# First experts of a decoder kernel: the norm of four tiles in two parts, and the shared up weights split in four pieces

## The chip, the cores and the metric

The kernel runs on one core of a Trainium2 chip. The time is the device time of the whole kernel in microseconds (us). TensorE multiplies 128-row tiles and writes to the accumulator memory PSUM (`PS` in the program, eight banks of 128x512 fp32); VectorE (DVE), ScalarE (ACT) and GpSimd (POOL) do the elementwise work; SyncE (SP) starts the DMA transfers. Each engine runs its own instruction list in order, and engines wait for each other on semaphores.

## The reference, cut to what matters

A decoder of two layers on 2048 rows of 512 features. Every sublayer is added to its input and normalised. The change lies in the third sublayer, the first experts:

```
probs = softmax(xt @ w_router);  top 4 of 128 experts
basis = silu(xt @ w_gate) * (xt @ w_up)          # 8 bases of 256
mixed = sum over the bases, weighted by the chosen experts
out   = mixed @ w_down
shared = (silu(xt @ shared_w_gate) * (xt @ shared_w_up)) @ shared_w_down
x = layernorm(x + out + shared)
```

Matrix products have to keep fp32 accuracy. So each operand is split in a high part, rounded to the format that TensorE takes, and a low part, the rest; a product is three matmuls (high by high, high by low, low by high).

## The kernel before, in words

`xN` holds the 2048 rows as 16 tiles of 128x512. Each sublayer is a function that returns one instruction list for each engine; `Norm` builds the layer norm for a group of tiles, with `st`, `mv`, `nv`, `ny`, `nc_` as small tiles of statistics that all norms share.

In the first experts the 8 bases go over 16 tiles each (128 "tile" steps, line 1123 on TensorE). Base k's weights are fetched to `sg[k % 2]` and split into `WH[k % 2]` by one ACT instruction (`split_w`, L1232) and into `WL[k % 2]` by one POOL instruction (L1400). The shared gate weights are k = 8, the shared up weights k = 9. `WH[1]` and `WL[1]` are in use by base 7 until its last matmul, so the split of the up weights can start no earlier than that.

Then the shared part goes over the 16 tiles. For each tile t TensorE runs, in this order:

- T(t): transposes of `mixed` (L1203) and of the shared product in `s2` (L1206) to PSUM;
- S(t+1): 12 matmuls of shared gate and 12 of shared up for the next tile (L1192);
- O(t): 18 matmuls of the down projection (L1219), which read `tH` and `tL`.

ACT copies T(t) into the high part `tH` (L1286, L1288), runs the silu of S(t+1) (L1278), and after tiles 3, 7, 11 and 15 applies the norm to four tiles (`apply_act`, L186). DVE writes the low part `tL` (L1380, L1383), the product with the shared up half (L1371), and adds O(t) to `xN` (L1390). After tiles 3, 7, 11 and 15 it works out the norm at once (`all_dve`): four statistics (L137), four aggregates (L141), two small operations (L145, L149), three Newton rounds of three small operations (L156, L157, L159) and the hand-over `nc` (L170), each small one waiting for the one before. ACT and DVE take their lists in order, so what stands behind the norm there, the copies and the low part of the next tile, waits for it. The order is written out by hand in the loops; PSUM banks are handed out by a table (`Rooms`) that the change leaves as it is.

Of the kernel before, what the change touches and what calls it, by code (L numbers as in the profile page):

```python
# [7 lines left out]
F32 = mybir.dt.float32  # L8
# [3 lines left out]
ALU = mybir.AluOpType  # L12
ACTF = mybir.ActivationFunctionType
AX = mybir.AxisListType

NT = 16
NP = 4
KC = 4
# [171 lines left out]
def pair3(hi, lo):  # L190

    return ((hi[0], hi[1]), (hi[0], lo[1]), (lo[0], hi[1]))
# [835 lines left out]
def experts0(K):  # L1028
# [3 lines left out]
    with ExitStack() as ph:  # L1032
        W = K.tensors(ph)
        XH, XL = W("bXH", [128, KC, 2048], F32R), W("bXL", [128, KC, 2048], F32R)
        sg = [W(f"sg{i}", [128, KC, 512]) for i in range(2)]
        WH = [W(f"WH{i}", [128, KC, 512], F32R) for i in range(2)]
        WL = [W(f"WL{i}", [128, KC, 512], F32R) for i in range(2)]
# [15 lines left out]
    for p in range(NP):  # L1053
# [10 lines left out]
    in_w = [K.dma("dma_x%d" % i, 5) for i in (0, 1)]  # L1064
    mix = K.flag("dve_mix", 1)
    r_hi, r_lo = K.flag("act_first_hi", 1), K.flag("dve_first_lo", 1)
    x_mm, x_hi, x_lo = K.flag("pe_turned", 16), K.flag("act_x_hi", 16), K.flag("dve_x_lo", 16)
    w_hi, w_lo = K.flag("act_w_hi", 10), K.flag("pool_w_lo", 10)
    d_hi, d_lo = K.flag("act_c_hi", 3), K.flag("pool_c_lo", 3)
    r_mm, r_out = K.flag("pe_route", 4), K.flag("act_route", 4)  # L1070
    c_mm, c_in, c_exp, c_gate = K.flag("pe_choose", 4), K.flag("dve_choose_in", 4), K.flag("act_choose", 4), K.flag("dve_gate", 4)
# [2 lines left out]
    t_mm, t_silu, t_mul, t_add = (K.flag("pe_basis", 8 * NT), K.flag("act_silu", 8 * NT), K.flag("dve_basis", 8 * NT),  # L1074
                                  K.flag("pool_mixed", 7 * NT))
    h_mm, h_silu, h_mul = K.flag("pe_shared", NT), K.flag("act_shared", NT), K.flag("dve_shared", NT)
    u_mm, u_hi, u_lo = K.flag("pe_out_turned", NT), K.flag("act_turned_hi", 2 * NT), K.flag("dve_turned_lo", 2 * NT)
    o_mm, o_add = K.flag("pe_out", NT), K.flag("dve_out_added", NT)
# [28 lines left out]
    def tensor(e):  # L1107
# [74 lines left out]
        def shared(t):  # L1182
            b, left = rooms["shared", t]
            for w in left:
                e.wait_ge(*w)
            for a, k in ((0, 8), (1, 9)):
                if t == 0:
                    e.wait_ge(*w_hi.upto(k + 1))
                    e.wait_ge(*w_lo.upto(k + 1))
                for kc in range(KC):  # L1190
                    for i, (x, w) in enumerate(pair3((XH, WH[k % 2]), (XL, WL[k % 2]))):
                        mm = e.matmul(PS[:, b + a, :], x[:, kc, 128 * t:128 * t + 128], w[:, kc, :],  # L1192
                                      start=kc == 0 and i == 0, stop=kc == KC - 1 and i == 2)
            mm.then_inc(h_mm.sem, 1)
# [27 lines left out]
    def scalar(e):  # L1222
        for w in ends:
            e.wait_ge(*w)

        def split_w(k):
            e.wait_ge(*in_w[k % 2].upto(k // 2 + 1))
            if k == 1:
                e.wait_ge(*r_mm.upto(NP))
            elif k:  # L1230
                e.wait_ge(*t_mm.upto(NT * (k - 1)))
            e.activation(WH[k % 2][:, :, :], sg[k % 2][:, :, :], ACTF.Copy).then_inc(w_hi.sem, 1)  # L1232

        def silu(n):
            if n >= 2:
                e.wait_ge(*t_mul.upto(n - 1))
            e.wait_ge(*t_mm.upto(n + 1))
            e.activation(s1[n % 2][:, 0:256], PS[:, rooms["tile", n][0], 0:256], ACTF.Silu).then_inc(t_silu.sem, 1)  # L1238

        e.wait_ge(*in_r.upto(1))  # L1240
        e.activation(rH, sg[1][:, :, 0:128], ACTF.Copy).then_inc(r_hi.sem, 1)
        split_w(0)
        for what, p in seq:
            if what == "turn":
                for kc in range(KC):
                    e.wait_ge(*x_mm.upto(4 * p + kc + 1))
                    e.activation(XH[:, kc, 512 * p:512 * p + 512], PS[:, rooms["turn", p, kc][0], :],
                                 ACTF.Copy).then_inc(x_hi.sem, 1)
            elif what == "route":
                if p:  # L1250
                    e.wait_ge(*c_mm.upto(p))
                e.wait_ge(*r_mm.upto(p + 1))
                e.activation(lT[:, :, :], PS[:, rooms["route", p][0], :].rearrange("p (a c) -> p a c", a=4),
                             ACTF.Copy).then_inc(r_out.sem, 1)
            elif what == "choose":
                e.wait_ge(*c_in.upto(p + 1))
                e.activation(pr[p % 2][:, :, :], pq[:, :, :], ACTF.Exp).then_inc(c_exp.sem, 1)
            elif what == "coef":
                e.wait_ge(*f_turn.upto(p + 1))
                e.wait_ge(*c_gate.upto(min(p + 2, NP)))  # L1260
                e.activation(pq[:, :, :], PS[:, rooms["coef", p][0], :].rearrange("p (a c) -> p a c", a=4),
                             ACTF.Copy).then_inc(f_out.sem, 1)
            elif what == "tile":
                silu(p)
        split_w(1)
        split_w(2)
        for k in range(1, 8):
            if k <= 3:
                e.wait_ge(*in_d.upto(k))
                e.activation(DH[:, 2 * k - 2:2 * k, :], sg[k % 2][:, 0:2, :], ACTF.Copy).then_inc(d_hi.sem, 1)  # L1270
            for t in range(NT):
                silu(NT * k + t)
            split_w(k + 2)

        def shared(t):
            e.wait_ge(*(h_mul.upto(t - 1) if t >= 2 else t_mul.upto(8 * NT - 1 + t)))
            e.wait_ge(*h_mm.upto(t + 1))
            e.activation(s1[t % 2][:, :], PS[:, rooms["shared", t][0], :], ACTF.Silu).then_inc(h_silu.sem, 1)  # L1278

        shared(0)  # L1280
        for t in range(NT):
            b = rooms["mixed", t][0]
            if t:
                e.wait_ge(*o_mm.upto(t))
            e.wait_ge(*u_mm.upto(t + 1))
            e.activation(tH[:, 0:2, :], PS[:, b, 0:256].rearrange("p (a c) -> p a c", a=2),  # L1286
                         ACTF.Copy).then_inc(u_hi.sem, 1)
            e.activation(tH[:, 2:6, :], PS[:, b + 1, :].rearrange("p (a c) -> p a c", a=4),  # L1288
                         ACTF.Copy).then_inc(u_hi.sem, 1)
            if t + 1 < NT:  # L1290
                shared(t + 1)
            if t % 4 == 3:
                norms[t // 4].apply_act(e)

    def vector(e):
        for w in ends:
# [67 lines left out]
                tile(p)  # L1364
        for n in range(NT, 8 * NT):
            tile(n)

        def shared(t):
            e.wait_ge(*(u_mm.upto(t - 1) if t >= 2 else t_add.upto(7 * NT - 1 + t)))
# [5 lines left out]
        for t in range(NT):  # L1375
            b = rooms["mixed", t][0]
            if t:
                e.wait_ge(*o_mm.upto(t))
            e.wait_ge(*u_hi.upto(2 * t + 1))
            e.tensor_tensor(tL[:, 0:2, :], PS[:, b, 0:256].rearrange("p (a c) -> p a c", a=2),  # L1380
                            tH[:, 0:2, :].bitcast(F32), ALU.subtract).then_inc(u_lo.sem, 1)
            e.wait_ge(*u_hi.upto(2 * t + 2))
            e.tensor_tensor(tL[:, 2:6, :], PS[:, b + 1, :].rearrange("p (a c) -> p a c", a=4),  # L1383
                            tH[:, 2:6, :].bitcast(F32), ALU.subtract).then_inc(u_lo.sem, 1)
            if t + 1 < NT:
                shared(t + 1)
            for w in came[t]:
                e.wait_ge(*w)
            e.wait_ge(*o_mm.upto(t + 1))
            e.tensor_tensor(xN[:, t, :], PS[:, rooms["out", t][0], :], xN[:, t, :], ALU.add).then_inc(o_add.sem, 1)  # L1390
            if t % 4 == 3:
                norms[t // 4].all_dve(e, step)

    def gpsimd(e):
        for w in ends:
            e.wait_ge(*w)

        def split_w(k):
            e.wait_ge(*w_hi.upto(k + 1))
            e.tensor_tensor(WL[k % 2][:, :, :], sg[k % 2][:, :, :], WH[k % 2][:, :, :].bitcast(F32),  # L1400
                            ALU.subtract).then_inc(w_lo.sem, 1)

        split_w(0)
        split_w(1)
        split_w(2)
        for k in range(1, 8):
            if k <= 3:
                e.wait_ge(*d_hi.upto(k))
                e.tensor_tensor(DL[:, 2 * k - 2:2 * k, :], sg[k % 2][:, 0:2, :],
                                DH[:, 2 * k - 2:2 * k, :].bitcast(F32), ALU.subtract).then_inc(d_lo.sem, 1)  # L1410
            for t in range(NT):
                n = NT * k + t
                e.wait_ge(*(t_add.upto(n - 2 * NT + 1) if k > 1 else scaled.upto(t + 1)))
                e.wait_ge(*t_mul.upto(n + 1))
                e.tensor_tensor(mixed[:, t, :], mixed[:, t, :], s2[n % 2][:, 0:256],  # L1415
                                ALU.add).then_inc(t_add.sem, 1)
            split_w(k + 2)

    def sync(e):
        for w in ends:  # L1420
# [19 lines left out]
                e.wait_ge(*d_lo.upto(k))  # L1440
            fetch(k + 2)

    K.ends = (o_mm.upto(NT), u_hi.upto(2 * NT), o_add.upto(NT), t_add.upto(7 * NT), w_lo.upto(10))
    return tensor, scalar, vector, gpsimd, sync


# [1442 lines left out]
```

## Time and profile before

| | |
|---|---|
| three runs, us | 2481.49, 2482.82, 2499.75 |
| median, us | 2482.82 |
| profiled execution, its own time, us | 2499.76 |
| its span, us | 2496.9 |
| mean granted TensorE clock | 0.910 |
| busy share: PE, DVE, ACT, POOL | 87%, 50%, 40%, 27% |
| the shared part of the first experts | 1426.95 to 1622.3 us of the span |

Times inside the span are counted from its first instruction. A row of the timeline gives the start, the duration, the engine, the line, and in brackets how long the engine stood idle before it and what ended that. TensorE's rows overlap, so its speed is read from start to start. PEclk in a row of windows is the granted clock: 1.00 is 2.4 GHz, and a stretch at 1.2 GHz counts 0.5.

### The profile page before, as it was taken

The numbers are of one execution on the slowest core, as the hardware profiler recorded it, in microseconds if no ns is written. First come the engines' busy times: TensorE is split into PE (matmuls) and PEld (weight loads), VectorE is DVE, ScalarE is ACT, GpSimd is POOL, SyncE is SP. The second block draws the span as 40 slices with busy tenths as digits, with TensorE's granted clock in tenths as the row PEclk, the third lists the DMA queues.
The fourth block names the chain that finished last, engine by engine and source line by source line (L and its number), as shares of the span: only waits on it lengthen the run. The fifth ranks groups of instructions, "written<-read, shape, count | busy, mean of one in ns | idle before, by whom it ended". The sixth has DMA issues, their size and how long they took to land. (4 is left out here: it accounts for less than half of the span.)

```text
span 2496.9 us, 36997 instructions
## 1 busy us (share of the span) xinstructions
PE 2163.4 (87%) x13655; PEld 1731.6 (69%) x13669; DVE 1256.4 (50%) x3242; ACT 997.4 (40%) x2273; POOL 684.8 (27%) x627
## 2 busy tenths in 40 slices
PE   7999999999997889689999999858989748888774
PEld 6789889889875666568888777746555337766542
DVE  2654554553565666551111123246777546676646
ACT  3322232232235666431111111135656527777632
POOL 2732342332311111114343300035444222232110
PEclk9999999999996666899999999968999969999886
DMA  4210010100002100101000000033323030000001
GB/s 138 91 35 30 22 35 30 28 32 22 22 1 74 38 27 1 56 9 51 34 34 17 1 1 1 1 65 60 54 46 60 9 118 14 27 14 10 1 9 67
DMA packets 41297, 86.43 MB, mean 35 GB/s; under 512 B 6176, under 2 KB 20768, under 8 KB 38176
## 3 DMA queue, kind: packets, MB, share of 16 engines
q1 hardware_dynamic: 41120, 84.08, 12.0%
q8 instruction: 110, 1.80, 0.3%
q14 instruction: 67, 0.55, 0.1%
HBM read 63.55 MB, written 4.26 MB: 27 GB/s over the span
## 5 line engine op out<-in xcount | busy, mean ns | idle before, releaser
L1123 PE MATMUL PS<-WH,bXH 128*128 128x512 f32 x512 | 201.6, 394 | 5.4 <-POOL WL L1400 5.4
L1123 PE MATMUL PS<-WL,bXH 128*128 128x512 f32 x512 | 201.0, 393 | 0.0
L1123 PE MATMUL PS<-WH,bXL 128*128 128x512 f32 x512 | 200.9, 392 | 0.0
L1805 DVE TENSOR_REDUCE aM<-PS 128x4 f32<-128x1024 f32 x128 | 155.1, 1222 | 49.8 <-PE PS L1645 48.8
L1318 DVE SCALAR_TENSOR_TENSOR s<-s,cf,PS 128x256 f32<-128x256 f32 x112 | 53.9, 481 | 250.5 <-ACT s L1238 241.5
L1238 ACT ACTIVATE s<-PS 128x256 f32<-128x256 f32 x128 | 49.3, 385 | 280.1 <-PE PS L1123 280.1
L1748 ACT ACTIVATE aPT<-PS 128x1024 f32<-128x1024 f32 x128 | 129.5, 1024 | 70.2 <-PE PS L1665 69.2
L307 PE MATMUL PS<-aXH,QKH 128*128 128x512 f32 x384 | 154.0, 401 | 0.0
L307 PE MATMUL PS<-aXH,QKL 128*128 128x512 f32 x384 | 151.7, 395 | 0.0
L307 PE MATMUL PS<-aXL,QKH 128*128 128x512 f32 x384 | 151.5, 395 | 0.0
L506 ACT ACTIVATE sq<-PS 128x768 f32<-128x768 f32 x64 | 52.0, 812 | 209.0 <-PE PS L397 163.4
L1415 POOL TENSOR_TENSOR mixed<-mixed,s 128x256 f32<-128x256 f32 x112 | 82.2, 737 | 186.1 <-DVE s L1318 186.1
L579 DVE TENSOR_TENSOR qkL<-PS,qkH 128x512 fp32r<-128x512 f32 x96 | 65.9, 690 | 127.5 <-ACT qkH L477 127.5
L2300 ACT ACTIVATE xP<-PS,xM 128x256 f32<-128x256 f32 x256 | 118.2, 483 | 21.2 <-DVE xM L2419 21.2
L638 POOL TENSOR_SCALAR E<-lgB,lgS 128x256 f32<-128x256 f32 x64 | 73.9, 1154 | 190.5 <-DVE aT L598 181.0
L559 DVE TENSOR_TENSOR xN<-PS,xN 128x512 f32<-128x512 f32 x128 | 87.9, 691 | 63.1 <-PE PS L341 59.5
L477 ACT ACTIVATE qkH<-PS 128x512 fp32r<-128x512 f32 x96 | 57.0, 598 | 150.1 <-PE PS L307 150.1
L1123 PEld LDWEIGHTS PS<-WH,bXH 128*128 128x128 f32 x512 | 97.2, 190 | 25.7 <-issue 5.5
L598 DVE TENSOR_TENSOR aT<-sq,E 128x512 f32<-128x512 f32 (+1 forms) x128 | 76.6, 640 | 71.0 <-ACT sq L506 42.0
L1123 PEld LDWEIGHTS PS<-WL,bXH 128*128 128x128 f32 x512 | 97.3, 190 | 20.3
L1123 PEld LDWEIGHTS PS<-WH,bXL 128*128 128x128 f32 x512 | 97.2, 190 | 20.3
L2419 DVE CUSTOM_DVE_ANT_0 PS<-PS,xmk 128x256 f32<-128x256 f32 x256 | 100.5, 456 | 16.2 <-PE PS L2190 15.8
(400 smaller groups left out, 6161.0 us busy)
## 6 DMA issues: line engine op xcount, KB each, us to landing
lgB<-gate_sums SPq DMA_DIRECT2D x32, 256.0 KB, 3.7
sg<-in_gu SPq DMA_DIRECT2D x8, 1024.0 KB, 4.7
aqs<-aQH SPq DMA_DIRECT2D x64, 128.0 KB, 4.2
gQK<-in_Wqk SPq DMA_DIRECT2D x8, 768.0 KB, 5.9
xN<-in_xT SPq DMA_DIRECT2D x4, 1024.0 KB, 12.0
gC<-in_Wc SPq DMA_DIRECT2D x8, 512.0 KB, 4.9
xN<-in_x SPq DMA_DIRECT2D x4, 1024.0 KB, 7.1
cst<-in_cT SPq DMA_DIRECT2D x8, 512.0 KB, 4.7
```

The costliest lines, as they stand in the source:

```text
L307: mm = e.matmul(PS[:, b, :], w[:, kc, 128 * m:128 * m + 128], x[:, kc, 512 * p:512 * p + 512], start=kc == 0 and i == 0, stop=kc == KC - 1 ...
L477: e.activation(qkH[:, m, :], PS[:, b, :], ACTF.Copy).then_inc(q_hi.sem, 1)
L559: e.tensor_tensor(xN[:, t, :], PS[:, b, :], xN[:, t, :], ALU.add).then_inc(o_add.sem, 1)
L579: e.tensor_tensor(qkL[:, m, :], PS[:, rooms["qk", n, m][0], :], qkH[:, m, :].bitcast(F32), ALU.subtract).then_inc(q_lo.sem, 1)
L598: at = e.tensor_tensor(aT[:, j, c:c + w].rearrange("p (h q) -> p h q", h=2), sq[:, c:c + w].rearrange("p (h q) -> p h q", h=2), E[:, j:j + ...
L638: e.tensor_scalar(E[:, j, 0:256], lgB[:, n % 2, 256 * j:256 * j + 256], lgS[:, c0:c0 + 1], 0.0, ALU.subtract, ALU.min)
L1123: mm = e.matmul(PS[:, b, :], x[:, kc, 128 * t:128 * t + 128], w[:, kc, :], start=kc == 0 and i == 0, stop=kc == KC - 1 and i == 2)
L1415: e.tensor_tensor(mixed[:, t, :], mixed[:, t, :], s2[n % 2][:, 0:256], ALU.add).then_inc(t_add.sem, 1)
L1748: e.activation(PT[:, n % 8, :, :], PS[:, b:b + 2, :], ACTF.Exp, scale=0.25).then_inc(t_exp.sem, 1)
L1805: e.tensor_reduce(M[j % 2][:, :, :].rearrange("x q (h c) -> x h q c", h=2)[:, :, :, i], PS[:, b:b + 2, :].rearrange("p h (q k) -> p h q k" ...
L2300: last = e.activation(P[:, i % 2, a, q, :], PS[:, r, 256 * q:256 * q + 256], ACTF.Exp, bias=M[y][:, q, h:h + 1], scale=-1.0, accum_out=den ...
L2419: last = e.tensor_tensor_reduce(out=s, in0=s, in1=mk[y][:, q, :], scale=1.0, scalar=3.0e38, op0=ALU.add, op1=ALU.min, accum_out=M[y][:, q, ...
```

## The change

Two edits, both in `experts0`.

The norm of tiles 0 to 3 is worked out in two parts. After tile 3, DVE takes the statistics and the seed with the first Newton round; after tile 4 it runs the other two Newton rounds and the hand-over, and ACT applies the norm then, behind tile 4's copies. The same goes for tiles 4 to 7 and 8 to 11. The norm of tiles 12 to 15 stays whole.

The split of the shared up weights becomes four ACT pieces and four DVE pieces of 128x512, and POOL no longer has a part in it. TensorE waits for each piece before the three matmuls that read it.

```diff
+    up_hi, up_lo = K.flag("act_first_hi", KC), K.flag("dve_first_lo", KC)
-    w_hi, w_lo = K.flag("act_w_hi", 10), K.flag("pool_w_lo", 10)
+    w_hi, w_lo = K.flag("act_w_hi", 9), K.flag("pool_w_lo", 9)
...
             for a, k in ((0, 8), (1, 9)):
-                if t == 0:
+                if t == 0 and a == 0:
                     e.wait_ge(*w_hi.upto(k + 1))
                     e.wait_ge(*w_lo.upto(k + 1))
                 for kc in range(KC):
+                    if t == 0 and a:
+                        e.wait_ge(*up_hi.upto(kc + 1))
+                        e.wait_ge(*up_lo.upto(kc + 1))
...
-            split_w(k + 2)
+            if k < 7:
+                split_w(k + 2)
+        e.wait_ge(*in_w[1].upto(5))
+        e.wait_ge(*t_mm.upto(8 * NT))
+        for kc in range(KC):
+            e.activation(WH[1][:, kc, :], sg[1][:, kc, :], ACTF.Copy).then_inc(up_hi.sem, 1)
...
-            if t % 4 == 3:
-                norms[t // 4].apply_act(e)
+            if t >= 4 and t % 4 == 0:
+                norms[t // 4 - 1].apply_act(e)
+        norms[NP - 1].apply_act(e)
...
+        for kc in range(KC):
+            e.wait_ge(*up_hi.upto(kc + 1))
+            e.tensor_tensor(WL[1][:, kc, :], sg[1][:, kc, :], WH[1][:, kc, :].bitcast(F32),
+                            ALU.subtract).then_inc(up_lo.sem, 1)
...
-            if t % 4 == 3:
-                norms[t // 4].all_dve(e, step)
+            if t % 4 == 3 and t + 1 < NT:
+                norms[t // 4].stats(e, step)
+                norms[t // 4].seed(e, step)
+            elif t >= 4 and t % 4 == 0:
+                norms[t // 4 - 1].newton(e, step)
+                norms[t // 4 - 1].hand_over(e)
+        norms[NP - 1].all_dve(e, step)
```

The DVE list behind the sum of tile 3, before (`tL` of tile 4 stands behind the whole norm):

```order
L1390 TENSOR_TENSOR xN<-PS,xN 128x512
L137 BN_STATS st<-xN 128x6 x4
L141 BN_AGGR mv<-st 128x2 x4
L145 TENSOR_SCALAR nv<-mv 128x4
L149 TENSOR_SCALAR ny<-nv 128x4
L156 TENSOR_TENSOR na<-ny 128x4
L157 SCALAR_TENSOR_TENSOR nb<-na,nv 128x4
L159 SCALAR_TENSOR_TENSOR ny<-nb,ny 128x4
```

After the three rounds and L170 come L1380 and L1383, `tL` of tile 4. The same place now, from the end of the first round on:

```order
L159 SCALAR_TENSOR_TENSOR ny<-nb,ny 128x4
L1394 TENSOR_TENSOR tL<-PS,tH 128x256
L1397 TENSOR_TENSOR tL<-PS,tH 128x512
L1385 TENSOR_TENSOR s<-s,PS 128x512
L1404 TENSOR_TENSOR xN<-PS,xN 128x512
L156 TENSOR_TENSOR na<-ny 128x4
L157 SCALAR_TENSOR_TENSOR nb<-na,nv 128x4
L159 SCALAR_TENSOR_TENSOR ny<-nb,ny 128x4
```

L1394 and L1397 are now `tL` of tile 4, L1385 its neighbour's product, L1404 the sum of tile 4. Two Newton rounds and the hand-over stand behind that sum, ahead of `tL` of tile 5.

ACT around the first norm, before (tile 3's copies, the silu of S(4), the four applications, tile 4's first copy):

```order
L1286 ACTIVATE tH<-PS 128x256
L1288 ACTIVATE tH<-PS 128x512
L1278 ACTIVATE s<-PS 128x512
L186 ACTIVATE xN<-xN,nc,ny 128x512 x4
L1286 ACTIVATE tH<-PS 128x256
```

and now:

```order
L1295 ACTIVATE tH<-PS 128x256
L1297 ACTIVATE tH<-PS 128x512
L1287 ACTIVATE s<-PS 128x512
L1295 ACTIVATE tH<-PS 128x256
L1297 ACTIVATE tH<-PS 128x512
L1287 ACTIVATE s<-PS 128x512
L186 ACTIVATE xN<-xN,nc,ny 128x512 x4
L1295 ACTIVATE tH<-PS 128x256
```

The four applications moved behind tile 4's copies and the silu behind them, ahead of tile 5's copies.

## Rows read from the trace of the kernel before

**Rows 1.** The page: the chain that ended last, shares of the span by engine.
```profile
PE 22%; issue 6%; DVE 6%; ACT 5%; POOL 2%; DMA 1%; SPq 0%; ACTq 0%; DVEq 0%; POOLq 0%
```

**Rows 2.** Waits of TensorE, 1426 to 1622 us: total, times, longest.
```profile
PE PS L1219 <- ACT tH L1288: 15.4, 4, 4.5
```

**Rows 3.** The chain in order of time, shared part: start, duration, what.
```profile
1457.45 4.08 PE PS L1219 x18
...
1472.39 5.47 PE PS L1192 x24
1477.86 4.08 PE PS L1219 x18
...
1492.57 6.69 PE PS L1219 x18
...
1505.37 4.08 PE PS L1219 x18
...
1601.04 4.08 PE PS L1219 x18
```

**Rows 4.** Timeline of DVE around the first norm: start, duration, instruction, idle before.
```profile
1471.85 0.69 DVE L1390 TENSOR_TENSOR xN<-PS,xN 128x512 f32<-128x512 f32 x1 [2.70 <-PE PS L1219]
...
1486.38 0.16 DVE L159 SCALAR_TENSOR_TENSOR ny<-nb,ny 128x4 f32<-128x4 f32 x1
...
1487.76 0.16 DVE L170 SCALAR_TENSOR_TENSOR nc<-mv,ny 128x4 f32<-128x4 f32 x1
1491.25 0.42 DVE L1380 TENSOR_TENSOR tL<-PS,tH 128x256 fp32r<-128x256 f32 x1 [3.33 <-ACT tH L1286]
1491.66 0.69 DVE L1383 TENSOR_TENSOR tL<-PS,tH 128x512 fp32r<-128x512 f32 x1
```

**Rows 5.** Timeline of TensorE's weight loads, the first of O(3) and of O(4).
```profile
1477.47 0.19 PEld L1219 LDWEIGHTS PS<-DH,tH 128*128 128x128 f32 x1
...
1492.53 0.29 PEld L1219 LDWEIGHTS PS<-DH,tH 128*128 128x128 f32 x1 [4.89 <-issue]
```

**Rows 6.** Timeline of TensorE: shared gate's last matmul, shared up's last, S(1)'s first.
```profile
1429.44 0.39 PE L1192 MATMUL PS<-WH,bXL 128*128 128x512 f32 x1
...
1438.95 0.63 PE L1192 MATMUL PS<-WH,bXL 128*128 128x512 f32 x1
...
1441.54 0.48 PE L1192 MATMUL PS<-WH,bXH 128*128 128x512 f32 x1
```

**Rows 7.** Timelines of ACT, DVE and POOL at the split of the up weights.
```profile
1427.49 1.91 ACT L1232 ACTIVATE WH<-sg 128x2048 fp32r<-128x2048 f32 x1
...
1427.70 0.48 DVE L1318 SCALAR_TENSOR_TENSOR s<-s,cf,PS 128x256 f32<-128x256 f32 x1 [2.24 <-ACT s L1238]
...
1429.48 4.50 POOL L1400 TENSOR_TENSOR WL<-sg,WH 128x2048 fp32r<-128x2048 f32 x1 [0.41 <-ACT WH L1232]
```

**Rows 8.** Router weights' split, 128x512: durations in ns (least, median, most).
```profile
L1241 ACT ACTIVATE WH<-sg x1: 613/613/613, 1025.8 to 1025.8; 128x512 fp32r<-128x512 f32 x1
...
L1307 DVE TENSOR_TENSOR WL<-sg,WH x1: 693/693/693, 1026.4 to 1026.4; 128x512 fp32r<-128x512 f32 x1
```

**Rows 9.** Timelines of TensorE at three short gaps.
```profile
1058.69 0.47 PE L1149 MATMUL PS<-bXH,WH 128*128 128x512 f32 x1 [1.55 <-DVE bXL L1326]
...
1441.12 0.66 PE L1206 MATMUL PS<-idF,s 128*128 128x128 f32 x4 [1.30 <-DVE s L1371]
...
1751.99 0.50 PE L1665 MATMUL PS<-aqs,aks 50*128 50x512 f32 x2 [1.30 <-DVE aM L1805]
```

**Rows 10.** Windows: stretch, busy us (instructions) by engine, PEclk, DMA share, GB/s.
```profile
1057.00:1060.00 3.00, 1.45 (x8) 1.12 (x7) 2.84 (x5) 1.88 (x4) 0.00 (x0) 1.00 0.00 0
1488.00:1498.00 10.00, 5.50 (x15) 4.35 (x15) 1.70 (x3) 4.11 (x7) 0.00 (x0) 0.66 0.00 0
1753.60:1757.00 3.40, 3.40 (x19) 1.71 (x21) 3.12 (x10) 1.70 (x4) 0.00 (x0) 0.51 0.08 27
1622.00:2497.00 875.00, 659.39 (x5284) 470.66 (x5296) 554.76 (x1449) 490.69 (x1074) 247.30 (x224) 0.88 0.17 40
```

More of the change, by code:

```diff
@@ L1416, in gpsimd @@
                                 ALU.add).then_inc(t_add.sem, 1)
-            split_w(k + 2)
+            if k < 7:
+                split_w(k + 2)
     def sync(e):
@@ L1441, in sync @@
             fetch(k + 2)
-    K.ends = (o_mm.upto(NT), u_hi.upto(2 * NT), o_add.upto(NT), t_add.upto(7 * NT), w_lo.upto(10))
+    K.ends = (o_mm.upto(NT), u_hi.upto(2 * NT), o_add.upto(NT), t_add.upto(7 * NT), w_lo.upto(9), up_lo.upto(KC))
     return tensor, scalar, vector, gpsimd, sync
```

## The prediction

> **What bounds the kernel now.** I read the page first, then the waits and the chain of the shared part, then the timelines of single engines. The page's chain of waits gives TensorE the largest part of the end [rows 1], and in the shared part TensorE is nearly the only member of the chain. So what counts there is when TensorE stands still. It stands still at two kinds of places.
>
> The first is the norm. One tile of the shared part takes 10.205 us when nothing is late: two of them lie between the O blocks at 1457.45 and 1477.86. From O(3) at 1477.86 to O(13) at 1601.04 there are 123.18 us for ten tiles, where 102.05 would do [rows 3]. The missing 21.1 us are the three norms. The first shows how 7.1 of them come about: O(3) to O(5) takes 27.51 us instead of 20.41. O(4) starts 4.50 us late (14.71 after O(3)), and then its 18 matmuls take 6.69 us instead of 4.08, 2.61 more [rows 3]. That second part is the clock: in 1488 to 1498 it was granted at 0.66 of 2.4 GHz, so part of the stretch ran at 1.2 GHz, after the stand [rows 10]. The table of waits names what is late: O waits for ACT's high part `tH`, 15.4 us in four waits, 4.5 at most [rows 2]; three are norms. `tH` of tile 4 stands on ACT behind the norm's application, which waits for the whole of DVE's norm.
>
> The second is the split of the shared up weights. The last matmul of shared gate starts at 1429.44; shared up waits for one POOL instruction of 4.50 us, which starts at 1429.48 behind one ACT instruction of 1.91 us [rows 6, 7]. Its 12 matmuls then run at the low clock, so that its last starts at 1438.95, and S(1) begins at 1441.54 [rows 6].
>
> **The norm in two parts.** The operations are the same ones in number and size; only their places change. Two places can now be late.
>
> Tile 4. DVE's last operation of the first part starts at 1486.38 (L159). The seven steps from there to `nc` at 1487.76 are 0.197 us each, so `tL` of tile 4 can start at 1486.58; ACT has its `tH` long done, since nothing of the norm stands before it. `tL` is 0.42 and 0.69 us, ready at 1487.69 [rows 4]. From the end of `tL` (1491.66 + 0.69 = 1492.35) to the first weight load of O(4) at 1492.53 it took 0.18, so the load comes at 1487.87. The unhindered place is 1477.47 + 10.205 = 1487.68 [rows 4, 5]. Late by 0.2 us.
>
> Tile 5. DVE adds O(4) (0.69 us), runs six steps (6 x 0.197 = 1.18) and starts `nc`. From `nc` (1487.76) to the weight load of the next O (1492.53) is 4.77 us: that holds ACT's application of four tiles, both copies and `tL`, the same list in the same order as now behind tile 5. Together 6.64 us after the sum's start. Undisturbed it is 5.62 (sum at 1471.85, load at 1477.47) [rows 4, 5]. Late by 1.0 us. This is the new wait: behind ACT's application stand tile 5's copies, and O(5) waits for them. Tile 6 has its usual room again.
>
> So each norm costs 1.2 us in place of about 7.0. Will a gap of 1.0 us lower the clock? Zero is one bound, and the 2.61 us behind the first norm's gap of 4.5 is the other. A gap of 1.55 us was followed by matmuls in a window granted at 1.00, and so was the gap of 1.30 at 1441.12, behind which the tile times are already the full 10.205 [rows 3, 9, 10]. But behind another gap of 1.30 us, at 1751.99, the clock is at 0.51 from 1753.6 [rows 9, 10]. That one lies in a stage that also runs many small matmuls; these gaps lie between two blocks of dense ones, as the first two do. I take zero, and keep 2.6 each for a rival. The Trainium skill (TensorE: Matmul & The Clock Gate, section "Why this matters for your kernels") asks only that gaps stay below about 3 us; by that rule the sum would be the same with no doubt left, and the gap at 1751.99 speaks against trusting it alone.
>
> Sum for the norm: 21.1 - 3 x 1.2 = **17.5 us** won.
>
> **The up split in four.** ACT starts at 1427.49. The same instruction on 128x512 took 0.613 us [rows 7, 8]; even without overlap the four pieces end at 1428.1, 1428.7, 1429.3, 1429.9. DVE is free at 1428.18, after its last product (1427.70 + 0.48). One piece there is 0.693 us, from the same operation on the router weights: ends 1428.9, 1429.6, 1430.3, 1431.0 without overlap [rows 7, 8]. TensorE wants them from 1429.67 on (1429.44 and one stride of 5.47/24 = 0.228) every 0.68 us: 1429.67, 1430.35, 1431.03, 1431.7 [rows 3, 6]. Each piece is there 0.7 us early. I cost the pieces at nothing; the cover is the second half of shared gate, and were it gone, the first piece would cost its 0.613 and 0.693, and the others, as long as their three matmuls, next to nothing. POOL loses 4.5 us of work and nobody waited for POOL otherwise. The six waits that TensorE gets extra are met when it comes to them.
>
> Shared up's last matmul then starts at 1429.44 + 12 x 0.228 = 1432.17 instead of 1438.95. From there to S(1) it was 2.59 us, of which the matmul 0.63; at full clock it is 0.39 [rows 6], so S(1) begins at 1432.17 + 2.59 - 0.24 = 1434.5 instead of 1441.54. **7.0 us** won. The gap behind shared up, for the silu and the product, stays and is 1.3 us [rows 9].
>
> Nothing else moves: no DMA is issued elsewhere, the last norm and the next stage's first waits are as before, and what is gained in the shared part passes to the end unless the clock of later stages falls otherwise.
>
> **Sum.** 17.5 + 7.0 = 24.5 us. The profiled execution, at 2499.76, would come to 2475.3. It lies 16.9 us above the median of the three runs, which I cannot place in one trace; the two edits are priced by engine durations that both share. So from the median: 2482.8 - 24.5 = **2458.3 us**, 0.99% less. What a measurement of this kernel can tell from no change is about 1%, here 24.8 us, so the forecast sits on that line.
>
> **The rivals.**
>
> 1. The clock falls at the new gaps. For it speaks the gap at 1751.99, against it the other two [rows 9]. Three gaps of 1.0 us at 2.6 each take back 7.8: 2466. If the 0.2 us gaps did it too, 15.7: 2474. Chance 0.12.
> 2. The later stages take another share of low clock. From 1622 to the end PEclk is 0.88 in 875 us, so some 210 us run at 1.2 GHz [rows 10], set by gaps of attention whose place relative to the clock's changes is not fixed. A shift of 16 us of such stretches is worth 8 us either way: 2450 or 2466. The spread of the three runs, 18 us, says that something of this size exists. Chance 0.2, somewhat more below than above, since shorter gaps leave fewer low stretches in the shared part itself too.
> 3. The cut does not free O. If the second part were as late for O(5) as the whole was for O(4), the stall would only move one tile on, and 7.0 from the split remain: 2475.8. Against it: the statistics and a third of the steps are done a tile earlier. It would need an application that starts over 3 us later than counted. Chance 0.04.
> 4. Slower. The one mechanism I see is again the low clock in later stages, pushed up by the earlier start. It decides when it costs more than 24.5 us, that is 49 us more at 1.2 GHz on top of 210; for 1% slower it takes 99 us more, half as much again. Twice those 49 us: 2482.8 - 24.5 + 49 = 2507. Nothing in the profile points that way. Chance 0.03.
>
> My forecast has 0.61; its own range is 2455 to 2462, from the steps rounded here and a gap of 1.0 us that may be 0.2 more or less at three places. The range that should hold the time 8 times in 10 takes in rivals 1 to 3, and the upper of the levels that the runs before show (2499.75 - 24.5 = 2475): 2448 to 2476.
>
> Of the forecast's 0.61 about half lies beyond 24.8 us, of rival 2 a little over half. Faster by over 1%: 0.42. Within 1%: 0.55. Slower: 0.03.
>
> **What would show it.** Shared up's matmuls follow shared gate's without a gap and at full clock, and no POOL instruction stands there. O(3) to O(5) takes 21.6 us instead of 27.5. TensorE's waits for `tH` in the shared part are about 1 us at tiles 5, 9 and 13 and 1.9 at tile 15 as before (15.4 less three of 4.5), with 0.2 at tiles 4, 8 and 12 behind DVE's `tL`. PEclk stays at 1.00 from the second tile to the last. From 1426.95 to the last O the shared part is 24.5 us shorter. The prediction is wrong if PEclk falls behind the gaps of 1.0 us (rival 1), if O(5) waits over 2 us (rival 3), or if the shared part shrinks as said and the whole does not (rivals 2 and 4).

## The result and the profile after

| | before | changed |
|---|---|---|
| median of four runs each, us | 2491.28 | 2460.32 |
| lowest and highest, us | 2481.49, 2507.09 | 2448.03, 2471.21 |
| profiled execution: own time, span, us | 2499.76, 2496.9 | 2452.88, 2449.9 |
| ratio with its 95% interval | | 0.9872 (0.9829 to 0.9914) |

The change makes the kernel faster: by the ratio 1.3%, 31.9 us of 2491.3, with an interval from 21 to 43. The forecast time was 2458.3. Ratios leave out executions more than 1.5% above the fastest of their kernel; there are none in this timing. The spans of the two profiles differ by 47.0 us, and not all of that is the change. I cut both into stages at TensorE's first instruction of each:

| us | before | changed |
|---|---|---|
| up to the cross attention | 754.7 | 752.4 |
| cross attention | 265.1 | 247.7 |
| first experts ahead of the shared part | 407.2 | 405.4 |
| shared part | 196.3 | 170.9 |
| all behind it | 873.7 | 873.5 |

Only the shared part holds edited work, and it is 25.4 us shorter; 24.5 were forecast. The chain in order of time there (start, duration, what), with the rows that answer to [rows 3]; lines have moved, so that L1223 is L1219 of before and L1196 is L1192:

```profile
1449.43 4.08 PE PS L1223 x18
1454.17 5.47 PE PS L1196 x24
1459.64 4.12 PE PS L1223 x18
1464.41 5.47 PE PS L1196 x24
1470.46 4.37 PE PS L1223 x18
1475.48 5.47 PE PS L1196 x24
1480.95 4.08 PE PS L1223 x18
...
1564.38 4.08 PE PS L1223 x18
```

O(4) starts 10.21 us after O(3), as if there were no norm. O(5) starts 10.82 after O(4), 0.6 late, and its 18 matmuls take 4.37 instead of 4.08, 0.3 more. From O(3) to O(14) it is 114.95 us, where before it was 133.39 (1477.86 to 1611.25 in the chain) and eleven undisturbed tiles would be 112.26. So 18.4 us came from the norms, and 0.9 each is left.

What is left, on ACT and DVE around tile 4's sum (timelines; the hand-over is L170, the application L186), against [rows 4]:

```profile
1463.86 0.69 DVE L1404 TENSOR_TENSOR xN<-PS,xN 128x512 f32<-128x512 f32 x1 [2.74 <-PE PS L1223]
1464.47 0.15 DVE L156 TENSOR_TENSOR na<-ny 128x4 f32<-128x4 f32 x1
...
1465.64 0.16 DVE L170 SCALAR_TENSOR_TENSOR nc<-mv,ny 128x4 f32<-128x4 f32 x1
1469.14 0.42 DVE L1394 TENSOR_TENSOR tL<-PS,tH 128x256 fp32r<-128x256 f32 x1 [3.34 <-ACT tH L1295]
```
```profile
1465.84 2.93 ACT L186 ACTIVATE xN<-xN,nc,ny 128x512 f32<-128x512 f32 x4 [5.50 <-DVE nc L170]
1468.68 0.36 ACT L1295 ACTIVATE tH<-PS 128x256 fp32r<-128x256 f32 x1
```

DVE waits 3.34 us for ACT's copy, and the copy stands behind four applications. The Newton steps begin 0.61 us after the sum's start, not 0.69, since they overlap its end.

The waits of TensorE in the shared part (total, times, longest), against [rows 2]: the long ones are gone, and the one that stays is the last tile's.

```profile
PE PS L1223 <- ACT tH L1297: 1.9, 1, 1.9
PE PS L1223 <- issue: 1.8, 3, 0.6
PE PS L1210 <- DVE s L1385: 1.3, 1, 1.3
```

The split, in the timelines of ACT, DVE, POOL and TensorE, against [rows 6, 7]. Shared up's first matmul starts at 1408.24, one stride behind shared gate's last; S(1) starts at 1413.08, 7.56 us after S(0)'s first at 1405.52. Before it was 14.59.

```profile
1406.06 2.18 ACT L1282 ACTIVATE WH<-sg 128x512 fp32r<-128x512 f32 x4
```
```profile
1406.72 3.04 DVE L1379 TENSOR_TENSOR WL<-sg,WH 128x512 fp32r<-128x512 f32 x4
```
```profile
1406.89 1.11 POOL L1434 TENSOR_TENSOR mixed<-mixed,s 128x256 f32<-128x256 f32 x1 [1.98 <-DVE s L1328]
```
```profile
1408.02 0.39 PE L1196 MATMUL PS<-WH,bXL 128*128 128x512 f32 x1
1408.24 0.39 PE L1196 MATMUL PS<-WH,bXH 128*128 128x512 f32 x1
...
1413.08 0.47 PE L1196 MATMUL PS<-WH,bXH 128*128 128x512 f32 x1
```

### The profile page after: what moved, and what is told of

It reads as the page before. It is cut to its first block, busy times and chain, and to the rows that moved or that the text cites. A ratio compares the mean times of both kernels' runs of the same rounds, so it can differ in the third digit from the quotient of the medians.

```text
span 2449.9 us, 37024 instructions
## 1 busy us (share of the span) xinstructions
PE 2133.2 (87%) x13669; PEld 1705.2 (70%) x13669; DVE 1259.3 (51%) x3246; ACT 997.3 (41%) x2276; POOL 680.5 (28%) x626
## 4 chain that ended last, share of the span: by engine, by line
PE 39%; issue 14%; DVE 7%; ACT 5%; POOL 4%; DMA 1%; SPq 0%; ACTq 0%; DVEq 0%; POOLq 0%
PE PS L1124 14%; PE PS L1196 4%; PE PS L1601 3%; PE PS L1223 3%; PE PS L1697 3%; ACT xP L2320 2%; PE PS L1665 2%; PE PS L2173 1%; DVE aM L1825 1%; DVE st L137 1%; PE PS L1685 1%; POOL xN L1009 1%; ACT xN L186 1%; PE PS L1652 1%; PE PS L2223 1%
```

## The experiments

Two stretches carry the readings: N, from O(3) to O(14), and P, from S(0)'s first matmul to S(1)'s. Both are read from start to start, N in the chain or to 0.1 us in the timeline. For one profile of each kernel:

| us | P | N | shared part |
|---|---|---|---|
| before | 14.6 | 133.4 | 196.3 |
| before, second profile | 13.7 | 132.7 | 194.7 |
| changed | 7.6 | 115.0 | 170.9 |
| changed, second profile | 7.6 | 115.0 | 172.5 |
| norm only | 14.5 | 114.9 | 179.4 |
| up split only | 7.6 | 132.0 | 187.9 |
| application later, DVE whole | 7.6 | 116.1 | 173.7 |
| four Newton rounds more | 7.6 | 122.0 | 178.0 |
| application in halves | 7.6 | 112.4 | 168.3 |
| low pieces on POOL | 10.1 | 114.9 | 173.3 |
| split whole, on DVE | 11.4 | 114.9 | 174.7 |
| halves and early statistics | 7.6 | 112.3 | 168.4 |

**Each edit alone.** The norm's edits without the up split:

```diff
-            if t % 4 == 3:
-                norms[t // 4].all_dve(e, step)
+            if t % 4 == 3 and t + 1 < NT:
+                norms[t // 4].stats(e, step)
+                norms[t // 4].seed(e, step)
+            elif t >= 4 and t % 4 == 0:
+                norms[t // 4 - 1].newton(e, step)
+                norms[t // 4 - 1].hand_over(e)
...
```

> Only the norm in two parts; the up split stays one ACT and one POOL instruction. If the two edits add up, O(3) to O(14) takes 114.95 us as with the whole change (133.39 before) and from S(0) to S(1) 14.6 as before. The shared part, first S(0) matmul to the next stage's first transpose, then takes 196.3 - 18.4 = 177.9 us. If instead the split's earlier finish helped the norms, O(3) to O(14) is longer than 114.95. What the whole kernel gains beyond 18.4 us comes from elsewhere: the stages ahead of the first experts, 17.4 us shorter in the profile after, should come out anywhere between the two values seen if their time is the clock's, and near the lower if the edit has to do with it.

And the up split without the norm's edits (the diff of the change without the rows on norms):

```diff
...
+        for kc in range(KC):
+            e.activation(WH[1][:, kc, :], sg[1][:, kc, :], ACTF.Copy).then_inc(up_hi.sem, 1)
...
```

> Only the up split in four pieces; the norm whole after tiles 3, 7, 11. From S(0) to S(1) 7.56 us as with the whole change, O(3) to O(14) 133.4 as before, the shared part 196.3 - 7.0 = 189.3 us. The rival: with the matmuls of shared up at full clock the norms cost something else (another place relative to the changes of the clock), which would show as an O(3) to O(14) more than 1 us away from 133.4.

N and P add up: each moves with its own edit alone. The timed ratios are 0.9937 (0.9897 to 0.9977) and 0.9953 (0.9914 to 0.9991); their gains add to 1.1%. Two expectations missed by about 1.5 us. With the norm alone the shared part is 1.5 longer than forecast, and the chain shows it in the last O, which took 4.38 in the changed kernel's first profile:

```profile
1588.55 0.93 issue
1589.48 5.98 PE PS L1219 x18
```

PEclk is 0.81 from 1588 to 1597 there, where the first profile of the changed kernel has 1.00 in its whole shared part. With the up split alone N is 1.4 shorter than 133.4, because the O blocks behind the first two norms took 5.96 and 5.93 us instead of 6.69 and 6.62. The kernel before, profiled again without any edit, also has a 5.95 there (behind its first norm). So the rival in the second expectation is not needed: what the clock takes at one and the same stand differs from run to run, here between 1.85 and 2.61 us (O blocks of 5.93 to 6.69 us for 4.08).

**Which of the two lists mattered.** DVE keeps the whole norm after tile 3, ACT applies it behind tile 4:

```diff
-            if t % 4 == 3 and t + 1 < NT:
-                norms[t // 4].stats(e, step)
-                norms[t // 4].seed(e, step)
-            elif t >= 4 and t % 4 == 0:
-                norms[t // 4 - 1].newton(e, step)
-                norms[t // 4 - 1].hand_over(e)
+            if t % 4 == 3:
+                norms[t // 4].all_dve(e, step)
```

> The change, but DVE works the norm out whole after tile 3 (7, 11) and only ACT's application moves behind tile 4. Theory: before, O(4) was late by the sum of DVE's norm and ACT's application, and ACT's place in the order is most of the 7 us. DVE's tL of tile 4 then stands behind the whole norm (nc at 1487.76, tL 0.42 + 0.69, 0.18 to the load: 1489.2 for 1487.7), so O(4) is 1.5 us late and O(5) not at all: O(3) to O(14) 112.3 + 3 x 1.5 = 116.8 us, clock at 1.00. Rival: the cut in DVE's list is what counts; then O(4) stays late by over 4 us, with low clock, and the stretch takes about 133.

```profile
1465.12 4.08 PE PS L1223 x18
...
1476.33 4.37 PE PS L1223 x18
...
1581.25 4.08 PE PS L1223 x18
```

116.1: O(4) starts 1.0 us late (11.21 after O(3)), its matmuls take 0.3 more, and no other tile is late. The 1.5 us expected was too much. ACT's place alone gives 17.3 of the 18.4 us; the cut in DVE's list adds 1.2.

**Halves.** ACT applies two tiles behind tile 4 and two behind tile 5:

```diff
-            if t >= 4 and t % 4 == 0:
-                norms[t // 4 - 1].apply_act(e)
+            if t >= 4 and t % 4 < 2:
+                norms[t // 4 - 1].apply_act(e, t % 4)   # two of the four tiles
```

> The change, and ACT applies the norm to two of the four tiles behind tile 4 and to the other two behind tile 5. The wait ahead of O(5) is the time of four applications (2.93 us) behind the hand-over; with two (1.5) the load can come 5.1 us after the sum's start, inside the undisturbed 5.62. O(3) to O(14) then takes 112.3 to 112.6 us instead of 114.95. Rival: what is left of the stall is DVE's Newton steps or the first part at tile 4; then the stretch stays at 114 to 115.

112.4, where eleven undisturbed tiles would take 112.26: the 0.9 us per norm came from the length of the application, and less than 0.1 each is left. The chain at the same place:

```profile
1463.24 4.08 PE PS L1223 x18
1467.98 5.47 PE PS L1196 x24
1473.45 4.14 PE PS L1223 x18
1478.24 5.47 PE PS L1196 x24
1483.71 4.08 PE PS L1223 x18
```

**A wider gap.** In the second part of the norm:

```diff
-                norms[t // 4 - 1].newton(e, step)
+                norms[t // 4 - 1].newton(e, step, 6)
```

> The change with four Newton rounds more in the second part of each norm (12 small DVE steps, 2.36 us), so that the gap ahead of O(5), O(9), O(13) grows from 0.9 to 3.3 us. Does a gap of this size lower the clock? If it does at all three, O(3) to O(14) takes 114.95 + 7.1 + 3 x 2.6 = 129.8 us; if at none, 122.0.

122.0, three times not. TensorE stood still for 2.9 us ahead of O(5), O(9) and O(13), not for the 3.3 expected, and each then ran at full clock. The first of them:

```profile
1478.68 4.10 PE PS L1223 x18
1491.83 4.37 PE PS L1223 x18
```
```profile
PE PS L1223 <- ACT tH L1297: 10.7, 4, 2.9
```

**The up split: pieces and engine.** The same four low pieces on POOL:

```diff
-        for kc in range(KC):     # in DVE's list
+        for kc in range(KC):     # in POOL's list
             e.wait_ge(*up_hi.upto(kc + 1))
             e.tensor_tensor(WL[1][:, kc, :], sg[1][:, kc, :], WH[1][:, kc, :].bitcast(F32),
...
```

> The change, with the four low pieces of the up weights on POOL instead of DVE. A POOL subtraction of 128x512 took 1.28 us elsewhere; POOL is free 2.1 us after S(0) begins (its last sum), so the pieces end 3.4, 4.7, 6.0 and 7.2 us after it, where TensorE wants the first at 2.7. Each piece paces three matmuls: from S(0) to S(1) 7.56 + 2.6 = 10.2 us, with no fall of the clock. If cutting alone did it and not the engine, 7.6 to 8.

And whole, one ACT and one DVE instruction:

```diff
-        for kc in range(KC):
-            e.activation(WH[1][:, kc, :], sg[1][:, kc, :], ACTF.Copy).then_inc(up_hi.sem, 1)
+        e.activation(WH[1][:, :, :], sg[1][:, :, :], ACTF.Copy).then_inc(up_hi.sem, 1)
...
```

> The change, with the up weights split whole: one ACT instruction (1.91 us) and one DVE instruction (2.3 us by the rows for 512 and 1056 elements, 0.693 and 1.259). Shared up starts 2.2 us late: from S(0) to S(1) 9.8 us, and 12.3 if that gap lowers the clock. If only the engine mattered and not the cut, 7.6 to 8.

POOL: 10.1. Its timeline has the pieces 5.01 us long together, and TensorE waits 0.61 ahead of the first and 0.30 ahead of the others. Whole on DVE: 11.4, between the two expected values, since the clock fell for part of the matmuls only:

```profile
1437.53 0.47 PE L1196 MATMUL PS<-WH,bXH 128*128 128x512 f32 x1 [2.04 <-DVE WL L1377]
1437.84 0.43 PE L1196 MATMUL PS<-WL,bXH 128*128 128x512 f32 x1
1438.07 0.63 PE L1196 MATMUL PS<-WH,bXL 128*128 128x512 f32 x1
1438.50 0.63 PE L1196 MATMUL PS<-WH,bXH 128*128 128x512 f32 x1
```

So both count: neither pieces on POOL (2.5 us) nor DVE without pieces (3.9, part of it the clock) hides the split.

**The rest of the 47 us.** The kernel before, unchanged, and the changed one again:

> The kernel before, unchanged, for a second profile. If the stages ahead of the first experts vary by the clock alone, the stage ahead of them (754.7 to 1019.8 us in the profile before, 265.0 us; 247.7 after) takes some other value between 245 and 265, while O(3) to O(14) is 133.4 and S(0) to S(1) 14.6 again within 0.5. If those 17 us belonged to the change, it takes 265 again.

> The changed kernel once more, timed against the kernel before. By the shared part alone it is 25.4 us shorter, 0.9898 of 2487.5; the first timing gave 0.9872 with an interval from 0.9829 to 0.9914. If what the first profile showed beyond 25.4 us was the clock of the stage ahead, which varies from run to run, the ratio comes out nearer to 0.990, and the shared part takes 170.9 us, or 172.5 if the clock falls at the gap before the last O; if it belonged to the change, near 0.981.

The cross attention took 258.1 us in the second profile of before and 255.9 in that of the changed kernel. 258.1 lies in the range that I gave it, 245 to 265, but the stage moves further than that: the kernel with low pieces on POOL showed 230.4 there and the whole split 269.8. In that second profile of before, P is 13.7 and N 132.7, 0.9 and 0.7 below the first, where I had allowed 0.5: again the clock, since fewer of the matmuls behind the same stands ran slow. No edit touches the cross attention. DVE's and ACT's busy time in it differ by some 3 us at most, TensorE's by 53, and the granted clock goes with it (windows: stretch, busy us (instructions) for PE, PEld, DVE, ACT, POOL, PEclk, DMA share, GB/s; of before, changed, POOL pieces, whole split):

```profile
754.70:1019.80 265.10, 222.12 (x1793) 170.57 (x1793) 162.48 (x677) 153.31 (x588) 47.90 (x34) 0.66 0.10 33
```
```profile
752.40:1000.10 247.70, 199.07 (x1792) 153.30 (x1793) 162.40 (x677) 152.51 (x588) 47.96 (x34) 0.75 0.11 35
```
```profile
754.80:985.20 230.40, 173.63 (x1793) 134.32 (x1793) 161.78 (x677) 151.74 (x588) 47.93 (x34) 0.86 0.12 38
```
```profile
755.40:1025.20 269.80, 226.57 (x1792) 173.26 (x1792) 164.92 (x677) 153.04 (x588) 47.81 (x34) 0.65 0.10 32
```

In the 19 timed executions of before that go with the first two experiments the total goes with the mean clock as well, from 2457.9 us at 0.933 to 2505.9 at 0.905.

The second timing gave 0.9877 (0.9830 to 0.9924), nearer to the 0.990 of the expectation than to its 0.981. 25.4 us of 2489.5 are 0.9898, inside both intervals. Both medians came out some 5 us lower than that; whether there is anything behind these 5 us stays open.

**Both savings in one version.** Halves, and the last norm's first three statistics taken behind their own sums:

```diff
-        norms[NP - 1].all_dve(e, step)
+            if 4 * NP - 4 <= t < 4 * NP - 1:
+                e.wait_ge(*o_add.upto(t + 1))
+                e.bn_stats(K.st[:, t % 4, :], xN[:, t, :]).then_inc(step.sem, 1)
+                step.n += 1
+        norms[NP - 1].stats(e, step, 3)     # only the fourth tile's
+        norms[NP - 1].seed(e, step)
+        norms[NP - 1].newton(e, step)
+        norms[NP - 1].hand_over(e)
```

> The halves kernel, and the statistics of tiles 12, 13 and 14 are taken right behind their sums, so that after the last sum only one of the four (0.69 us) stands there instead of all (2.46). O(3) to O(14) stays at 112.4 us. From the next stage's first transposes to its first projection it was 19.2 us; ACT's application starts 1.8 us earlier, and the weight split behind it then waits for it or for the weights' transfer, whichever is last (the transfer landed 0.1 us before the application began in the profile after and would now be the later start): 17.4 to 17.9 us. Against the changed kernel 2.5 + 1.5 = 4 us less, against the one before 29.4 by the shared part, 0.988; the spread of the stage ahead lets the timed ratio come out anywhere from 0.983 to 0.993.

N is 112.3. From the start of the last sum to the next stage's weight split it is 8.1 us (1583.26 to 1591.39) instead of 10.4 (1575.50 to 1585.86 in the changed kernel), 2.2 us less. That is more than expected: up to the next stage's first projection it is 17.0 us, below the 17.4 to 17.9. The statistics gave 1.6 us; the other 0.6 came from one small DVE operation, L149, which took 0.34 us instead of 0.97 (last section). The median is 2443.85 us against 2489.51, ratio 0.981 (0.9761 to 0.9858), also below the 0.983 to 0.993 expected. It is faster than the kernel before. That it is faster than the changed kernel too is shown by the stages of the profiles, 2.5 us in the shared part and 2.2 behind it, and not by the timing, where the two intervals overlap. All behind the shared part took 865.8 us, 7.7 less than in the changed kernel's first profile. 2.2 of them are the edit; 5.3 lie behind the next stage's first projection, in a stretch that took 373.5 to 374.8 us in the eleven other profiles and 368.2 in this one. Why is open, and there is only this one profile.

## Why the prediction was right

**The time and the gain.** That the time came out 2.0 us from the forecast is partly luck. The medians lie 31.0 us apart where 24.5 were forecast, and the median of before had moved from 2482.82 (three runs) to 2491.28 (four); the two nearly cancel. What the prediction can be held to is the shared part: 25.4 us for 24.5.

**What bounds.** That TensorE's stands in the shared part pass to the end one for one held: all behind the shared part took 873.7 and 873.5 us.

**The norm.** Forecast 17.5, measured 18.4. The mechanism is the forecast one, with both new places as named. The term for tile 4 was 0.2 us for the weight load; the matmuls showed 0.0, since the loads run ahead of them. The term for tile 5 was 1.0; O(5) starts 0.6 late and 0.3 follows. The late start of the weight load, 0.95 (6.57 us after the sum's start for 5.62), was over-counted by the 0.08 us by which the steps overlap the sum. Together 0.9 instead of 1.2. The later experiment shows what I had not separated: nearly all of the gain comes from ACT's place in the order, and the cut of DVE's norm, the edit that names the change, is worth 1.2 us.

**The clock at the new gaps (rival 1).** Taken as zero, and it was: at the 0.6 us of the changed kernel, at 1.0 us ahead of O(4) with DVE's norm whole, and at 2.9 us with the longer Newton part. But it is the gap that was there before, 1.9 us ahead of the last O, that the clock fell behind in three profiles of twelve. I had looked at the new gaps only.

**The up split.** Forecast 7.0, measured 7.0. The cover was thinner than said, at the second piece. The first took 0.69 us and was ready at 1407.41, 0.8 us ahead of TensorE. The second took 1.23, beside POOL's last sum, and was ready at 1408.56, 0.4 us ahead of its matmul at 1408.92 and not 0.7. The prediction had POOL out of the split, and so did not ask what POOL's last sum would do to DVE there.

**The later stages (rival 2).** I had placed the unsteady clock behind the change, by PEclk 0.88 there [rows 10]. It sits ahead of it: in the profiles the cross attention takes 230 to 270 us, all behind the shared part 872.7 to 875.4, and 865.8 only in the last version. That the profiled execution of before lay 17 us above its median would fit: its cross attention took 7 us more than in the second profile and 35 more than in the shortest. The other executions of that timing left no profile, so it is not shown. The total changes with a stage that the change does not touch, so the chances, half and half around 1%, were about right for the timed total and too cautious for the work itself.

## What to carry to other kernels

Where two engines work in order, look for what stands between a long wait and the work that the bottleneck needs next: moving ACT's application one tile later gave 17 us without making anything shorter. Cut an operation into pieces only if each piece is as short as what it feeds, and give it to an engine that is free then. When a kernel's total scatters by more than the gain, compare the edited stage in two profiles each and let the total only agree.

## What the runs showed of the hardware

**A gap's length alone does not tell whether the clock falls.** In the shared parts of the twelve profiles, gaps of 2.9 us did not lower it in three of three, nor did 0.6, 1.0 or 1.3 us anywhere. The gap ahead of the last O, 1.9 to 2.0 us, did in three of twelve, and one of 2.04 us did once. Gaps of 4.5 us did in nine of nine, for 1.85 to 2.61 us, and the 4.3 us ahead of shared up in three of three. The 1.9 us gap has the short transposes right ahead of it, the 2.9 us gap has 24 dense matmuls. Whether that matters is not shown; ahead of the 1.9 us gap the work is the same in all twelve, and what followed was not. The Trainium skill (TensorE: Matmul & The Clock Gate, section "Why this matters for your kernels") asks for no gaps above about 3 us. The falls behind 4.3 and 4.5 us agree with that; the falls at 1.9 and 2.04 are below it. No gap between 2.9 and 4.3 us was run.

**DVE and POOL beside each other.** At the up split POOL's last sum took 1.11 us instead of 0.74. It starts at 1406.89, while DVE is in its first piece:

```profile
1406.72 0.69 DVE L1379 TENSOR_TENSOR WL<-sg,WH 128x512 fp32r<-128x512 f32 x1
```
```profile
1407.33 1.23 DVE L1379 TENSOR_TENSOR WL<-sg,WH 128x512 fp32r<-128x512 f32 x1
```

The first piece ends at 1407.41, POOL's sum at 1408.01, and the second piece, 1.23 us instead of 0.69, at 1408.56. So POOL's sum ends 0.60 us after the first piece and the second piece 0.55 us after POOL's sum, each a little less than it takes alone. With the pieces on POOL, where DVE has nothing beside it, the same sum took 0.74 us again.

In the last norm, while POOL fills `aks`, two DVE operations on 128x4 took 0.91 and 0.97 us instead of 0.17, in the profile after as in the one before. They end at 1579.93 and 1580.93; the two fills of the row below end at 1579.90 and 1580.90:

```profile
1578.95 1.95 POOL L1860 MEMSET aks<- 32x1024 f32 x2
```
```profile
1579.02 0.91 DVE L145 TENSOR_SCALAR nv<-mv 128x4 f32<-128x4 f32 x1
1579.96 0.97 DVE L149 TENSOR_SCALAR ny<-nv 128x4 int32<-128x4 int32 x1
1580.96 0.17 DVE L156 TENSOR_TENSOR na<-ny 128x4 f32<-128x4 f32 x1
```

In the last version the norm meets the fills at another place. There the second operation falls beside a short fill and ends with it, at 1586.50 for 1586.48:

```profile
1586.16 0.32 POOL L1869 MEMSET aV<- 128x256 f32 x1
```
```profile
1586.16 0.34 DVE L149 TENSOR_SCALAR ny<-nv 128x4 int32<-128x4 int32 x1
```

The Trainium skill (SBUF — State Buffer, section "Summary: rules for kernel authors") says that when DVE is in a 2-port mode, or has two SBUF inputs while the GpSimd instruction reads SBUF, the second of the two to issue is blocked until the first finishes. The ends above agree with that in all these cases; that the operations on 128x4 run in such a mode is not seen in a trace. The two small operations are 1.5 us longer than elsewhere, ahead of the next stage. The last version got 0.6 of it back by where it meets the fills; no run moved the fills away.
